# Moving the seventh value tile of an attention from the end of its opening into its first group

## What is computed

```python
def attention(x, wq, wk, wv, wo):          # H=16 query heads, KV=4 key heads, HD=128
    q = (x @ wq).reshape(b, s, H, HD)
    k = (x @ wk).reshape(b, s, KV, HD)
    v = (x @ wv).reshape(b, s, KV, HD)
    q = apply_rope(q, cos, sin)
    k = apply_rope(k, cos, sin)
    ...
    scores = jnp.einsum('bqhd,bkhd->bhqk', q, k) / np.sqrt(HD)
    ...
    probs = jax.nn.softmax(scores, axis=-1)
    out = jnp.einsum('bhqk,bkhd->bqhd', probs, v).reshape(b, s, H * HD)
    return out @ wo
...
x = x + 0.5 * ffn(layernorm(x))            # attention, then 8 experts, top 2
x = x + rwkv(layernorm(x))
x = x + 0.5 * ffn(layernorm(x))
```

## Time and profile before

| what | value |
|---|---|
| time, median of 3 runs | 1303.83 us (1302.98 to 1304.02) |
| time of the profiled execution | 1302.31 us |
| its span, first to last instruction | 1300.5 us |
| PE busy | 1137.3 us, 87% of the span |
| DVE busy | 962.7 us, 74% |
| ACT busy | 770.1 us, 59% |
| POOL busy | 600.9 us, 46% |
| mean granted TensorE clock | 0.932 of full |

### The profile page before, as it was taken

How to read it: one execution, slowest core, us unless ns; L and a number is a source line. 1 busy time by engine, 2 the same in 40 slices (tenths; PEclk the granted TensorE clock), 3 DMA queues, 4 the chain that set the end, 5 groups by cost and what they waited for, 6 DMA issues and landing times.

```text
span 1300.5 us, 18374 instructions
## 1 busy us (share of the span) xinstructions
PE 1137.3 (87%) x6320; PEld 965.3 (74%) x6320; DVE 962.7 (74%) x2057; ACT 770.1 (59%) x1510; POOL 600.9 (46%) x450
## 2 busy tenths in 40 slices
PE   5899999999997599963398789999999999749994
PEld 4688888888886488851277578888888888638883
DVE  6677887887887677648756768788787788667773
ACT  6666676666664177732453666666666666237772
POOL 4666666657600144522512366665775560014451
PEclk9899999999999599986788899999999999859997
DMA  4100100100108311134100200010000011911113
GB/s 132 38 1 2 37 1 1 38 1 2 49 1 306 110 42 53 49 101 130 53 1 1 69 1 1 1 37 1 12 27 1 1 49 46 326 49 49 50 53 117
DMA packets 48651, 66.27 MB, mean 51 GB/s; under 512 B 5808, under 2 KB 34352, under 8 KB 48432
## 3 DMA queue, kind: packets, MB, share of 16 engines
q1 hardware_dynamic: 42032, 50.94, 11.9%
q0 software_dynamic: 4416, 12.06, 3.1%
q10 hardware_dynamic: 2112, 2.10, 0.5%
HBM read 54.86 MB, written 10.22 MB: 50 GB/s over the span
## 4 chain that ended last, share of the span: by engine, by line
PE 77%; DVE 11%; ACT 5%; POOL 2%; issue 2%; DMA 2%; SPq 0%; ACTq 0%; DVEq 0%; POOLq 0%
PE ps L1423 20%; PE ps L1425 19%; PE ps L1424 19%; PE ps L1493 9%; PE ps L1553 6%; PE ps L1541 2%; POOL probs L723 1%; DVE h L1127 1%; PE ps L1561 1%; PE ps L1395 1%; PE ps L1524 1%; DVE mixT L1357 1%; ACT probs L791 1%; DVE ps L1105 1%; DMA mixT<-y_dram 1%
## 5 line engine op out<-in xcount | busy, mean ns | idle before, releaser
L791 ACT ACTIVATE probs<-ps,negmax 128x128 f32<-128x128 f32 (+7 forms) x256 | 189.6, 741 | 90.2 <-DVE negmax L1105 86.9
L797 ACT ACTIVATE probsT<-ps 128x512 fp32r<-128x512 f32 x288 | 170.2, 597 | 116.7 <-PE ps L1493 115.4
L1111 DVE TENSOR_TENSOR probsT<-ps,probsT 128x512 fp32r<-128x512 f32 x288 | 196.1, 685 | 48.8 <-ACT probsT L797 47.2
L1105 DVE CUSTOM_DVE_ANT_0 ps<-ps,causal 128x128 f32<-128x128 f32 (+7 forms) x256 | 193.2, 761 | 26.0 <-PE ps L1425 24.0
L647 POOL TENSOR_TENSOR crossed<-crossed,rope 128x512 f32<-128x512 f32 x70 | 91.1, 1301 | 195.6 <-ACT crossed L777 195.6
L1493 PE MATMUL ps<-square,probs 128*128 128x128 f32 x1152 | 171.2, 274 | 0.1
L694 POOL DMA_INDIRECT xs<-rows_dram,token_of x46 | 69.7, 1516 | 204.5 <-DVE token_of L1202 177.5
L1493 PEld LDWEIGHTS ps<-square,probs 128*128 128x128 f32 x1152 | 141.0, 140 | 30.4 <-DVE probsT L1111 3.0
L1210 DVE TENSOR_TENSOR parts<-experts,parts 128x1024 fp32r<-128x1024 f32 x92 | 112.3, 1226 | 49.7 <-ACT parts L837 49.2
L1127 DVE SCALAR_TENSOR_TENSOR h<-ps,rowinv,h 128x256 f32<-128x256 f32 x256 | 123.6, 483 | 33.4 <-PE ps L1425 26.3
L1423 PE MATMUL ps<-keysT,queriesT 128*128 128x512 f32 (+4 forms) x384 | 141.9, 370 | 3.2 <-DVE straight L1081 1.4
(11 more groups left out here) (238 smaller groups left out, 2832.1 us busy)
## 6 DMA issues: line engine op xcount, KB each, us to landing
experts<-in_L_ffn_w_dram SPq DMA_DIRECT2D x48, 512.0 KB, 7.6
w_in<-in_L_ffn_wq_dram SPq DMA_DIRECT2D x8, 512.0 KB, 3.9
wo_in<-in_L_ffn_wo_dram SPq DMA_DIRECT2D x8, 512.0 KB, 5.9
rows_dram<-probs ACTq DMA_DIRECT2D x4, 512.0 KB, 8.7
probs<-y_dram SPq DMA_DIRECT2D x8, 256.0 KB, 4.2
mixT<-y_dram SPq DMA_DIRECT2D x8, 256.0 KB, 4.8
probs<-in_L_attn_x_dram SPq DMA_DIRECT2D x2, 512.0 KB, 4.6
w_in<-in_L_ffn_wk_dram SPq DMA_DIRECT2D x8, 128.0 KB, 4.8
```

The lines of the kernel that those rows point to most:

```text
L791: act.activation(probs[:, i % 2, k, 0:w], ps[:, 2 * slot_n:2 * slot_n + 2, :].rearrange("p b n -> p (b n)")[:, at:at + w], ACT.Exp, bias=n ...
L797: act.activation(probsT[:, m % 3, 0, :], ps[:, 4 + m % 2, :], ACT.Copy).then_inc(S["probsT_high"], 1)
L1105: dve.tensor_tensor_reduce(out=row, in0=row, in1=causal[:, T - w:T], scale=-1.0, scalar=LARGEST, op0=ALU.add, op1=ALU.min, accum_out=negma ...
L1111: dve.tensor_tensor(probsT[:, m % 3, 1, :], ps[:, 4 + m % 2, :], probsT[:, m % 3, 0, :].bitcast(F32), ALU.subtract).then_inc(S["probsT_low ...
```

## The change

`v 6` leaves the hand-written list of the opening, and the planner gets it as a step of the first group, as it had `v 7` already. It must come behind `turn 0 0`, and `v 7` behind `v 6`. The program's waits for the step stay what they were, and no instruction is added or removed on PE. The planner gives the three engines new orders for the first steps of `SECOND`; from `project q1 3` on, the lists are the same as before. Both attentions use the list.

```diff
@@ -134,8 +134,8 @@
     if opening:
         for t in range(4, NT):
             place = t - 2.5 if t == NT - 1 else 0.1 + 0.25 * (t - 4)
-            if t == NT - 1:
-                add("PE", ("v", t, 0), 1.39, place)
+            if t >= 6:
+                add("PE", ("v", t, 0), 1.39, place, ("v", t - 1, 0), ("turn", 0, 0))
             add("ACT", ("v_high", t, 0), 0.6, place, ("v", t, 0), ("v_high", t - 1, 0))
             add("DVE", ("v_low", t, 0), 0.69, place, ("v_high", t, 0), ("v_low", t - 1, 0))
             for i in range(t, NT):
@@ -232,7 +232,7 @@
             pe += [("v", n - 2, 0)]
     for k in range(REP):
         pe += [("scores", i, k) for i in range(EARLY)]
-        pe += [("v", 3 + k, 0)]
+        pe += [("v", 3 + k, 0)] if k < REP - 1 else []
```

## The result

| kernel | median | from to | runs |
|---|---|---|---|
| before | 1303.53 us | 1302.15 to 1304.28 | 8 |
| with the change | 1297.59 us | 1295.27 to 1301.77 | 8 |

The ratio is 0.9957 (95% interval 0.9944 to 0.9970): 5.9 us faster in the medians, and between 3.9 and 7.3 us by the interval. The direction was forecast. Two later series of the same kernel gave 1298.87 us (5 runs) and 1297.56 us (12 runs). Against the 1303.4 us of the kernel before in those series, that is a gain of some 5.2 us.

A forecast was written before the change was run, and what follows sets the result against it. PE was taken to bound the kernel, busy for 87% of the span. Wait and order's 1.8 us plus the clock's 1.35 gave 3.15 us: 1300.7 us against the median 1303.83, range 1298.6 to 1303.2 us.

The forecast's parts named there:

- The wait: PE's idle time behind the opening's last scores: resumes 1.2 us earlier per attention, 1.8 us idle left, 2.4 us won.
- No wait at `v 6` and `turn 1 1`: In the first group, both waits are covered by 0.6 us at full clock, so they cost nothing.
- What is taken back: At `turn 2 0`: 0.7 us more wait, net 0.3 us per attention, twice 0.3 in all; 1.8 us stay.
- The clock: Half-clock stretches after PE's idle time in both attentions: 1.35 us won, bounds nothing and 4.5.
- rival 2: The clock never falls in either attention: all of 1.8 + 4.5 = 6.3 us won, 1297.5 us; chance 0.08.
- Rival 1: Clock gives nothing, falling for 3.4 us in both attentions; only the order's 1.8 us remain, 1302.0 us; chance 0.23.
- Rivals 3 and 4: Respectively: no gain, about 1303.8 us, chance 0.06; slower by a new wait at `turn 2 0`, 1309.7 us, chance 0.03.

The follow-up runs named there:

- new order, old wait: Changed kernel, but `turn 0 0` waits until value tile 2 has been split, as `v 6` did before: 1303.18 us, ratio 0.9999 to the kernel before.
- other banks: Kernel before in its order, value tiles 0 and 1 exchange PSUM banks, tile 6 takes tile 0's: 1296.45 us, ratio 0.9948 to the kernel before.
- experiment 2: Kernel before, with 12 matmuls that add to no result while PE waits ahead of `v 6`: 1298.53 us, ratio 0.9964 to the kernel before.
- experiment 3: Changed kernel, with 8 matmuls that add to no result in the remaining idle time: 1295.83 us, ratio 0.9939 to the kernel before.

## Why the prediction was wrong in its size

All profiled executions side by side. "Rest" is the time less both rulers.

| kernel | time, us | ruler 1 | ruler 2 | clock at half near the ruler's start, us | rest, us |
|---|---|---|---|---|---|
| before | 1302.31 | 37.24 | 36.25 | 6.8, 3.4 | 1228.8 |
| before again | 1304.63 | 37.30 | 37.01 | 6.8, 6.8 | 1230.3 |
| new order, old wait | 1302.27 | 37.31 | 36.54 | 6.8, 3.4 | 1228.4 |
| before, wait filled | 1297.14 | 34.72 | 34.70 | 0, 0 | 1227.7 |
| change | 1298.62 | 35.35 | 33.79 | 3.4, 0 | 1229.5 |
| change again | 1300.43 | 35.23 | 35.21 | 3.4, 3.4 | 1230.0 |
| change, third | 1300.27 | 35.20 | 35.22 | 3.4, 3.4 | 1229.9 |
| change, wait filled | 1297.33 | 33.72 | 33.71 | 0, 0 | 1229.9 |
| other banks | 1297.84 | 33.04 | 33.07 | 0, 0 | 1231.7 |

**The wait: right.** 1.2 us per attention were forecast; idle time went from 3.05 to 1.93 (0.1 more than the 1.8 forecast), released by the exp.

**No wait at `v 6` and `turn 1 1`: right.** Neither has idle time ahead of it, at half clock in the first attention and at full clock in the second.

**What is taken back: right.** 0.7 us of new wait at `turn 2 0` were forecast and 0.74 us stand there. The net was to be 0.9 us won per attention, and experiments 2 and 3 measure 1.0, so 0.1 was taken back in place of 0.3. The sum's 1.8 us for wait and order measured 2.0.

**The clock: this is the step that failed, by its size.** It was put at 1.35 us and measures about 1.9 by the ruler and 2.5 by the medians. "These two are all the trace has, so I take the middle" averaged the execution at hand (1.8 won) with a supposed one in which both attentions lose little before (0.9). The runs show the opposite neighbour. A second profile of before has the long half-clock stretch in both attentions, and against experiment 2 the profiles with 3.05 us idle lose 4.1 and 4.9 us to the clock. The three profiles of the change lose 1.7, 3.0 and 3.0 us against experiment 3, 2.6 in the mean. So about 1.9 us are won here by the ruler. By the medians it is more: the clock cost 4.9 us before (1303.39 to 1298.53) and 2.4 with the change (1298.2 to 1295.83), which is 2.5 us won; the two filled kernels have five runs each, up to 4.2 us apart, so this figure is good to a microsecond or so. The mechanism and its two sizes, 2.7 and 1.8 us for one attention, were near (2.5 and 1.5 by the ruler). With them, the unaveraged sum for the profiled execution, 1.8 + 1.8 = 3.6 us, would have been the better forecast.

**The range: too narrow.** Its lower end of 1298.6 us left out most of rival 2 and with it gains over 5.2 us against the 1303.83 us of the forecast (4.9 against the 1303.53 measured beside the change), although the clock's bound alone reached to 4.5 beside 1.8 for the order. Experiment 3, which has all of that, was expected at 1297.2 us and reached 1295.83.

**What stays open.** By the profiles the change is worth 2.0 + 1.9 = 3.9 us: the mean of the two rulers' sum is 73.9 us over two profiles of before and 70.0 over three of the change. The medians say 5.2. The rest of the program varies by 4 us between executions. One part is the start: the last scores of the opening end near 39.5 us in five of the nine profiles and near 40.7 in the other four; profiles of the kernel before and of the change are in both groups. The other is mainly the stretch between the two rulers, which these rows show for before and before again, then for the three profiles of the change (length, PE busy, granted clock, DMA):

```profile
76.61:750.07 673.46, 576.92 (x3200) 0.91 0.16 51
77.98:751.34 673.36, 576.21 (x3200) 0.92 0.16 51
76.03:748.64 672.61, 574.88 (x3200) 0.92 0.16 51
74.77:749.67 674.90, 579.63 (x3200) 0.91 0.16 50
74.73:749.34 674.61, 580.05 (x3200) 0.91 0.16 50
```

The same kernel takes 2.0 to 2.3 us longer there in the two executions with the lower clock. Over all 25 executions of the change, the 18 with a mean granted clock of 0.934 to 0.939 took 1295.27 to 1299.04 us, and the 7 with 0.931 took 1299.65 to 1301.77. Two of the three profiles are of these seven, and the third, too, is slower than the median. So the profiles show the changed kernel slower than it mostly is, and part of the 1.3 us between 3.9 and 5.2 can come from that. Whether in the other executions the clock falls less often at this place, or stays up longer elsewhere, no profile shows.

**The rivals.** Rival 1 (the clock gives nothing, 1302.0 us) had its first condition, 3.4 us at half clock in both attentions, in two of three profiles of the change. Its second fails: the kernel before loses 4.1 and 4.9 us, not 3.0. Rival 2 (the clock never falls) holds for one attention in six. By the Trainium skill's rule on idle gaps (TensorE: Matmul & The Clock Gate, "Why this matters for your kernels") all six should have kept the clock; the measurement decides against it for gaps of 1.93 us. That page's other statement ("What's actually happening"), that the point of change varies from run to run, agrees with the traces: around equal idle times of 1.93 us the fall came 1.4 to 1.7 us into them (four times), 0.5 us behind (once) or not at all (once). Rivals 3 and 4 need a wait that isn't there: the largest new one is 0.74 us.

## What to carry to other kernels

Price a wait of TensorE by its length and by what it does to the granted clock after it: here 3.05 us of idle time cost 1.5 to 2.6 us more afterwards. Several profiles of the same kernel tell how that second price varies (1.7 to 3.0 us per execution in three of the change), and a few matmuls put into the wait tell what it is; if they make the kernel faster, look for real work or for another buffer that ends the wait. When the release of one buffer holds an engine, look first whether another one is empty already: by the ruler two exchanged banks did more than the new order.

## What was unexpected of the hardware

An idle time of 1.93 us was enough for the granted clock to fall in five attentions of six, in four of them before PE resumed. With 3.05 us it fell in all six, either 1.3 to 2.0 us into the idle time or 1.4 us after its end. Each time it stayed at half for 3.4 or 6.8 us. Idle times of 0.56 and 0.72 us, 4 us apart, left it at full in the one profile taken. And 24 matmuls that compute nothing made the kernel 4.9 us faster (0.9964, 0.9950 to 0.9978).
